# Attention with gated decay: one weighing over two banks, and gate peaks by one subtraction and one masked product

## What is computed

```python
gi = concatenate([q, k, v]); ig = gi @ igate_w.T + igate_b; fg = gi @ fgate_w.T + fgate_b
cs = cumsum(log_sigmoid(fg))
log_D = where(tril, cs[..., :, None] - cs[..., None, :], -inf) + ig[..., None, :]
max_log_D = max(log_D, axis=-1)
D = exp(log_D - max_log_D)
C = (qh @ kh.T / sqrt(dh)) * D
h = C / (maximum(abs(C.sum(-1)), exp(-max_log_D)) + 1e-6) @ vh
```

## Time and profile before

| what | value |
|---|---|
| median of 3 runs | 3052.46 us (3051.99 to 3055.52) |
| span of the profiled execution | 3051.6 us |
| PE busy in it | 2948.7 us |
| DVE busy in it | 1819.7 us |
| ACT, POOL busy in it | 1132.8, 1065.5 us |
| `weighted_scores` (L1030) | 256 operations, 164.7 us |

### The profile page before, as it was taken

The page is one execution under the profiler, slowest core; times in us unless marked ns, Lnnn a source line. Parts: engine busy times, 40 slices in busy tenths (PEclk is TensorE's granted clock), DMA queues, the critical chain, the costliest instruction groups (busy, mean ns, idle before and its releaser), DMA issues.

```text
span 3051.6 us, 60802 instructions
## 1 busy us (share of the span) xinstructions
PE 2948.7 (97%) x24708; PEld 2395.3 (78%) x24708; DVE 1819.7 (60%) x5124; ACT 1132.8 (37%) x2025; POOL 1065.5 (35%) x1029
## 2 busy tenths in 40 slices
PE   6999999999997599999999999999999999999998
PEld 5888888888886477777777877787787787778886
DVE  6999999999998645354454444444434445444332
ACT  5788788787886211121121121122112122112110
POOL 4777777777776311111122111121112112121111
PEclk9999999999998699999999999999999999999999
DMA  3243444434443412241242132232123214222121
GB/s 122 100 160 120 162 139 149 161 123 165 141 134 113 131 40 37 35 99 31 46 99 48 36 80 35 37 96 62 31 38 93 41 31 111 38 50 57 35 37 24
DMA packets 140575, 250.71 MB, mean 82 GB/s; under 512 B 31968, under 2 KB 31968, under 8 KB 140296
## 3 DMA queue, kind: packets, MB, share of 16 engines
q1 hardware_dynamic: 106296, 170.80, 17.2%
q0 software_dynamic: 28672, 67.65, 12.6%
q10 hardware_dynamic: 5328, 8.36, 0.9%
HBM read 137.23 MB, written 101.19 MB: 78 GB/s over the span
## 4 chain that ended last, share of the span: by engine, by line
PE 64%; DVE 1%; DMA 1%; issue 0%; ACT 0%; POOL 0%; ACTq 0%; DVEq 0%; POOLq 0%
PE DN L1729 32%; PE UP L1700 30%; PE TT L1673 1%; DMA w_raw<-in_L_ffn_W_down 1%; DVE c_hit L1392 0%; PE c_bank L1385 0%; DVE down_lo L1258 0%; PE c_bank L1369 0%; DVE c_hit L1413 0%; ACT z L1643 0%; DVE c_within L1408 0%; ACT down_hi L1252 0%; POOL out_x L1618 0%; DVE c_gained L1445 0%; DVE mid_lo L1761 0%
## 5 line engine op out<-in xcount | busy, mean ns | idle before, releaser
L1618 POOL DMA_INDIRECT out_x<-y,slots x128 | 208.5, 1629 | 1621.1 <-DVE y L1785 1621.1
L1643 ACT ACTIVATE z<-UP,bup 128x512 f32<-128x512 f32 (+1 forms) x352 | 240.8, 686 | 1085.6 <-PE UP L1700 1066.5
L1729 PE MATMUL DN<-down_hi,mid_hi 128*128 128x512 f32 x1408 | 570.8, 405 | 0.0
L1700 PE MATMUL UP<-xT_hi,up_lo 128*128 128x512 f32 (+1 forms) x1408 | 555.5, 395 | 0.0
L1700 PE MATMUL UP<-xT_hi,up_hi 128*128 128x512 f32 (+1 forms) x1408 | 553.5, 393 | 1.8 <-DVE xT_lo L1740 0.9
L1700 PE MATMUL UP<-xT_lo,up_hi 128*128 128x512 f32 (+1 forms) x1408 | 552.0, 392 | 0.0
L1729 PE MATMUL DN<-down_hi,mid_lo 128*128 128x512 f32 x1280 | 505.8, 395 | 0.0
L1729 PE MATMUL DN<-down_lo,mid_hi 128*128 128x512 f32 x1280 | 505.7, 395 | 0.0
L1759 DVE CAST mid_hi<-z 128x512 fp32r<-128x512 f32 (+1 forms) x352 | 151.2, 429 | 486.4 <-ACT z L1643 486.4
L1783 DVE TENSOR_TENSOR y<-DN,bdn 128x512 f32<-128x512 f32 x128 | 88.5, 692 | 432.3 <-PE DN L1729 419.5
L1700 PEld LDWEIGHTS UP<-xT_hi,up_hi 128*128 128x128 f32 (+1 forms) x1408 | 260.3, 185 | 67.5 <-ACT z L1643 2.8
(11 more groups left out here) (264 smaller groups left out, 4971.9 us busy)
## 6 DMA issues: line engine op xcount, KB each, us to landing
xs<-in_x SPq DMA_DIRECT2D x64, 512.0 KB, 3.7
kraw<-in_ctx SPq DMA_DIRECT2D x32, 1024.0 KB, 7.3
out_x<-xs SPq DMA_DIRECT2D x32, 1024.0 KB, 12.5
rows_scratch<-xfb SPq DMA_DIRECT2D x32, 1024.0 KB, 10.6
w_raw<-in_L_ffn_W_down SPq DMA_DIRECT2D x40, 512.0 KB, 4.4
w_raw<-in_L_ffn_W_up SPq DMA_DIRECT2D x16, 682.5 KB, 4.1
mid_hi<-mid_hi ACTq DMA_DIRECT2D x32, 86.0 KB
mid_lo<-mid_hi ACTq DMA_DIRECT2D x32, 84.0 KB
```

Source lines behind the costliest of these rows:

```text
L1618: pool.indirect_dma_start(out_rows, bass.IndirectOffsetOnAxis(ap=slots[:, m:m + 1], axis=0), y[:, t, :], None, compute_op=ALU.add).then_in ...
L1643: act.activation(z[0:r, k % 2, :], UP[k % 3][0:r, :], ACT.Silu, bias=bup[0:r, e // 2, f:f + 1]).then_inc(s["z"], 1)
L1700: mm = pe.matmul(UP[k % 3][0:r, :], weights.up[wa][:, c, f * P:f * P + r], xT[xa][:, c, :], start=first, stop=(c == CH - 1 and wa == 1))
L1729: mm = pe.matmul(DN[m % 2][:, :], lhs, rhs, start=first, stop=(f == FCH - 1 and lhs is parts[-1][0]))
```

## The change

`weighted_scores` handles both banks of a pair in one operation on 128 x 1024, and counts once on `cc`. All that wait on `cc` are rewritten for one count a pair, so that a fill of either `QK` bank waits until both halves are weighed.

`gate_peaks` subtracts once on all 128 partitions, into `low`, and then writes the whole matrix of a batch by one product of `low`, repeated for the four tiles, and `own`, repeated for 128 columns. Between the two there is a wait on VectorE's own semaphore (`step`).

```diff
-                    weighted[kind, b, k] = (s["cc"], 2 * (PAIRS * (i - 2) + pair) + side - 1)
+                    weighted[kind, b, k] = (s["cc"], PAIRS * (i - 2) + pair + 1)
...
-                        pe.wait_ge(s["cc"], 2 * g)
+                        pe.wait_ge(s["cc"], g)
...
-                    pe.wait_ge(s["cc"], 2 * g + 2)
+                    pe.wait_ge(s["cc"], g + 1)
...
-                    for par in range(2):
-                        c = C[:, 2 * (g % CRING) + par, :]
-                        dve.scalar_tensor_tensor(out=c, in0=QK[:, par, :], scalar=DH ** -0.5, in1=c, op0=ALU.mult, op1=ALU.mult)\
-                           .then_inc(s["cc"], 1)
+                    c = C[:, 2 * (g % CRING):2 * (g % CRING) + 2, :]
+                    dve.scalar_tensor_tensor(out=c, in0=QK[:, :, :], scalar=DH ** -0.5, in1=c, op0=ALU.mult, op1=ALU.mult)\
+                       .then_inc(s["cc"], 1)
...
-                    for j in range(TILES):
-                        rows = slice(QD * j, QD * j + QD)
-                        ins = dve.scalar_tensor_tensor(out=peaks[rows, b % 2, j * P:(j + 1) * P], in0=run[rows, :], scalar=incoming[rows, :],
-                                                       in1=held[rows, 0, :].bitcast(FP32), op0=ALU.max, op1=ALU.subtract)
-                    ins.then_inc(s["xm"], 1)
+                    step(dve.scalar_tensor_tensor(out=low[:, :], in0=run, scalar=incoming, in1=held[:, 0, :].bitcast(FP32),
+                                                  op0=ALU.max, op1=ALU.subtract))
+                    dve.tensor_tensor(peaks[:, b % 2, :].rearrange("p (j n) -> p j n", n=P), spread(low[:, :], 1, TILES),
+                                      spread(own[:, :], 2, P), ALU.mult).then_inc(s["xm"], 1)
```

## The result

The changed kernel takes 3087.26 us (median of 4 runs, 3084.86 to 3087.83) where the kernel before takes 3053.33 us in the same rounds (4 runs): ratio 1.0104, 95% interval 1.009 to 1.0118. It is 34 us, 1.0%, slower. The forecast was 3088 us. The profiled execution has a span of 3085.4 us, 33.8 us above the 3051.6 of before.

The account below looks back on a forecast made before the run. Attention batches were taken as bound by TensorE and VectorE in alternating halves. Per batch +0.65 + 0.88 - 0.12 = +1.41 us; 27 x 1.41 - 1.6 = 36.5, rounded to 36, on 3052.5 gave 3088 us; range 3050 to 3098 (8 in 10).

Parts of the forecast that it names:

- The two halves of the batch: Attention batch: VectorE's savings in TensorE's half are worth nothing; its losses in its own half are paid one for one.
- The cap on gains: VectorE's half of a batch: gains are paid only up to TensorE's wait for the states, 0.43 us.
- The merged weighing: `weighted_scores`: 1.225 us for 1024 elements, saving 0.06 us a pair; pairs 3 and 0 count, -0.12 us a batch.
- The other effect: Merging brings `nn` 0.06 us earlier, and with it GpSimd's work until its column weights.
- the first meeting: Product in `gate_peaks` against GpSimd's first column weight: GpSimd 0.025 us ahead, product held, +0.65 us a batch.
- the second meeting: `sm_all` against GpSimd's first addition: VectorE 0.15 us behind, `sm_all` held, +0.88 us a batch.
- rival 2: GpSimd first at the peaks, but `sm_all` slips ahead of the addition: +0.53 us a batch, 3067 us; chance 0.10.
- The cover of the bank's release: TensorE's turn of `k` into pair 0's bank: released some 0.55 us later, 0.3 us cover, cost nothing.
- Rival 1: VectorE first at the peaks, `sm_all` held behind GpSimd's last column weight: +0.27 us a batch, 3059 us; chance 0.20.
- rival 4: Weighing across two banks gains nothing, so VectorE is first at the peaks: +0.39 us a batch, 3062; chance within Rival 1's.
- Rival 3: No meeting costs anything, for instance if broadcast inputs don't block: 0.43 us a batch regained, 3039 us; chance 0.14.
- The total: Whole kernel: 27 batches at +1.41 us less 1.6 us already lost today, 36.5 rounded to 36; chance 0.48.

Follow-up runs that it names:

- the kernel with the memset: The changed kernel with one memset of a 128 x 1 buffer on GpSimd ahead of its column weights: 3065.05 us, ratio 1.0035.

## Why the prediction was right

Point by point, with the profile after beside it:

- **The two halves of the batch.** Right. VectorE's losses in its own half were paid one for one: 30.56 - 29.16 = 1.40 us, against 1.41 in the sum. TensorE's wait for the states rose to 0.66 us, less than the "about 1 us or more" of the forecast, because another 0.6 us of its waiting came earlier, at the turn of `k` (below). The cap on gains is real too: 28.83 us is the least that any kernel here reached, 0.33 us below before, where I had put the cap at 0.43.
- **The merged weighing.** 1.22 us, as taken from the slope; no price for crossing a bank. The other effect, GpSimd 0.06 us earlier, was about 0.06 (in steady batches its column weights start 0.38 to 0.40 us after `held` ends, against 0.45 with the weighing put back), and it decided the first meeting, as the step said it might. On its own the edit was forecast nowhere; the run gives it -0.12 us a batch and nothing in the median.
- **The first meeting.** GpSimd first by 0.02 to 0.04 us (0.025 forecast); product 1.68 to 1.71 us (616.69 - 614.975 = 1.72 in the working); GpSimd's next 1.64 (1.64).
- **Two sizes were off and cancelled.** The weighing behind the product starts 0.07 to 0.08 us before the product's end; behind the quarters it started 0.03 us after. The peaks so cost +0.54 us, not +0.65. VectorE therefore came to `sm_all` only 0.04 us behind GpSimd's addition instead of 0.15, and was held for the whole of it: +1.0 us instead of +0.88. Sum 0.54 + 1.0 - 0.14 = 1.40. With 0.04 us less the second meeting could have gone the other way (rival 2), so the step that I gave 0.15 us of room had about a quarter of that. That it held is luck as much as working.
- **The cover of the bank's release.** 0.3 us of cover was named for TensorE's turn of `k`. With VectorE 1.4 us later there it was gone, and TensorE waits 0.6 us; it costs nothing visible, because TensorE still waits 0.66 us for the states behind it. The step left that wait out.
- **The rivals.** Rival 1 is real, in one batch of the changed kernel (29.44) and in two experiments (29.46 and 29.50 us, 11 us in all each, where the prediction had 6.5 with the merge's gain and, in rival 4, 9.5 without it). With the merge the batch was near the forecast (+0.30 against +0.27 us) by parts that cancelled: VectorE waits 0.3 us for ScalarE behind the last weighing (5.3 us in 18 batches of the kernel with the memset), which the prediction left out, and `sm_all` is then held by 0.5 us and not by 0.76. Rival 3's point, that repeated operands may not block, is refuted by the product of 1.69 us together with `low` in PSUM, where the same repeated operands take 0.69. Even without any hold its 13 us would not have come in full: the best kernels get 5 to 10 us of median.
- **The total.** It came nearer than its sum deserved. 27 x 1.41 - 1.6 gave 36.5 us; up to the experts' part the executions differ by 31.9 us. The last 26 distances of `held` add up to 761.3 us before and 793.4 after, 32 us and not 26 x 1.40 = 36.4: before has some 3 us in batches that take longer than its steady one, after has 1 us less than 26 steady ones, the batch of 29.44 being the main part. Another 2.0 us came behind the attention stage, where nothing was forecast; single runs of the kernel before lie 10 us apart beside the first experiments (3049 to 3059), so no cause need be sought for it.

Not settled: in all executions but that of the peaks alone, one to three batches have a gap of 0.44 to 1.1 us in TensorE's work that the profile puts down to no other engine, near 230, 520 or 805 to 845 us. Often VectorE and GpSimd then meet in another order for a batch or two. They may be part of why medians fall short of the steady batches; no run shows that, nor what makes them.

## What to carry to other kernels

Count the SBUF inputs of each VectorE instruction that runs beside GpSimd: the second one is what may be held, for nearly a whole GpSimd instruction, and a short operation loses as much as a long one (0.19 us became 1.19, 0.69 became 1.69). Moving one small operand into PSUM, or the operation itself into a stretch where GpSimd is idle, takes the hold away without changing the arithmetic. In a pipeline whose queues repeat with a fixed offset, an edit that shortens something by 0.06 us can turn such a meeting round in every round, so edits should be timed together and alone, and the start times of both engines be compared before one believes a sum of durations.

## What the runs showed of the hardware

The order at such a meeting is sharper than I had allowed for. In the prediction I left it open between VectorE 0.03 us ahead and 0.09 behind. Over the executions of before, after and the first four experiments (merge alone, peaks alone, `low` in PSUM, GpSimd later), `sm_all` or the product of the peaks, where it has two inputs in SBUF, starts within 0.25 us of a product or addition of GpSimd 187 times. In 109 of them it was ahead, or behind by at most 0.003 us, and took its usual time within 0.04 us; in 78 it was behind by 0.005 us or more and was held, by 0.8 us at least. The edge itself rests on few starts: 0.012 us ahead and 0.003 behind weren't held, 0.005 and 0.011 behind were, one time each. The Trainium skill, "SBUF — State Buffer", section "Who interferes with whom", says that the order of issue decides; the traces agree, by the starts they record. That the loser is blocked for the whole instruction, the Trainium skill says in the same section of VectorE's two-port modes; for the two SBUF inputs here the traces show a little less: the product of 0.69 us ended 0.54 us after GpSimd's instruction, `sm_all` of 0.19 us 0.05 us after it, both 0.14 us sooner than if they had begun at its end. The other way round, GpSimd works from about 0.14 us before a product of VectorE ends (1.64 us in place of 1.19, from 634.90 on, with the product ending at 635.49).

How closely instructions follow one another on VectorE differs with the partitions. Where two have nothing to wait for and both work on all 128, the second starts 0.08 us before the first ends: two weighings of 0.685 us last 1.29 together, and the merged weighing starts 0.08 us before the product's end. Where the next one starts at another partition, that overlap is gone: four quarters of 0.348 us last 1.43 us together, the next starting 0.01 us after the one before, and the weighing behind the last quarter starts 0.03 us after its end. So the four quarters took 0.07 us more than the sum of their durations until the weighing started, where one operation on 128 partitions takes 0.08 us less than its own.
